# A transformer block with polymax attention: the first attention iteration started from SBUF

## The reference

```python
x = x + 0.5 * ffn(layernorm(x))
x = x + attn(layernorm(x), W_attn, W_proj)
x = x + 0.5 * ffn(layernorm(x))
# ffn(x)  = x @ W.T + b + (x @ V_r) @ C.T          256 -> 256, rank 32
# attn(x) = y @ W_proj, 16 heads of 16 numbers, causal, no softmax but
# polymax(s) = (s*s + 1)/1000 for s > 0, (1 - s/100)/1000 for -100 <= s <= 0, else 0
```

## Time and profile before

| | us |
|---|---|
| median of 3 runs | 1990.86 (1988.06 to 1992.23) |
| the profiled execution, its own time | 1981.72 |
| its span in the profile | 1980.0 |
| PE / DVE / ACT / POOL busy | 1641.8 / 1264.8 / 1335.6 / 1325.6 |
| start of iteration 1 (first raise of its half 0) | 284.0 |
| start of iteration 2 | 390.1 |

### The profile page before, as it was taken

The page is one execution under the profiler, slowest core; times in us unless marked ns, Lnnn a source line. Parts: engine busy times, 40 slices in busy tenths (PEclk is TensorE's granted clock), DMA queues, the critical chain, the costliest instruction groups (busy, mean ns, idle before and its releaser), DMA issues.

```text
span 1980.0 us, 64621 instructions
## 1 busy us (share of the span) xinstructions
PE 1641.8 (83%) x27158; PEld 764.4 (39%) x27158; DVE 1264.8 (64%) x2065; ACT 1335.6 (67%) x1634; POOL 1325.6 (67%) x1419
## 2 busy tenths in 40 slices
PE   4677789798989788898878889787988888888874
PEld 2443334343434344343434434343443333334332
DVE  2456676666666667666666756667666667667552
ACT  2244567787777676777667677767777787776560
POOL 3354567787777767677776767867676767676551
PEclk9898999999999999999999999999999999999996
DMA  2344332323334152333415233341513232314111
GB/s 84 112 147 127 109 127 61 117 78 103 93 92 122 42 161 64 103 90 98 127 42 160 65 97 96 94 119 43 144 60 117 69 82 63 108 37 113 36 36 57
DMA packets 155175, 183.00 MB, mean 92 GB/s; under 512 B 22012, under 2 KB 129660, under 8 KB 152836
## 3 DMA queue, kind: packets, MB, share of 16 engines
q1 hardware_dynamic: 154884, 178.82, 30.7%
HBM read 102.43 MB, written 76.30 MB: 90 GB/s over the span
## 4 chain that ended last, share of the span: by engine, by line
PE 56%; DVE 15%; issue 11%; ACT 10%; POOL 4%; DMA 2%; SPq 0%; DVEq 0%; ACTq 0%; POOLq 0%
PE y_ps L974 21%; PE score L974 19%; PE bank L974 13%; DVE rp L909 8%; ACT rp L818 3%; PE bank L1000 3%; ACT rp L838 3%; ACT rp L834 2%; POOL z L685 2%; DVE lin L915 2%; ACT lin L824 1%; DVE bnst_ln L934 1%; DVE qk_max L921 1%; DMA out_dram<-x 1%; DVE rest L454 1%
## 5 line engine op out<-in xcount | busy, mean ns | idle before, releaser
L909 DVE TENSOR_SCALAR rp<-score 128x1024 f32<-128x1024 f32 (+2 forms) x864 | 860.2, 1002 | 321.6 <-PE score L974 313.3
L974 PE MATMUL score<-qs,ks 96*32 96x512 bf16 (+3 forms) x10240 | 711.4, 354 | 237.0 <-DVE rp L909 126.4
L723 POOL TENSOR_TENSOR rp<-rp 128x1024 f32<-128x1024 f32 (+1 forms) x416 | 756.7, 1828 | 170.5 <-DVE rp L909 158.8
L818 ACT ACTIVATE rp<-score 128x1024 f32<-128x1024 f32 (+1 forms) x416 | 413.0, 993 | 340.9 <-PE score L974 338.0
L974 PE MATMUL y_ps<-rp,vt 128*16 128x512 f32 (+3 forms) x5120 | 598.4, 540 | 9.0 <-ACT rp L838 7.3
L974 PEld LDWEIGHTS score<-qs,ks 96*32 96x32 bf16 x10240 | 241.5, 96 | 648.1 <-DVE rp L909 338.7
L834 ACT ACTIVATE rp<-rp,rise 128x1024 f32<-128x1024 f32 (+1 forms) x416 | 456.1, 1119 | 1.4 <-POOL rp L698 1.4
L698 POOL TENSOR_SCALAR_AFFINE_SELECT rp<-rp 128x256 f32<-128x256 f32 (+1 forms) x384 | 184.0, 481 | 315.4 <-ACT rp L818 165.4
L838 ACT ACTIVATE rp<-rp 128x1024 f32<-128x1024 f32 (+2 forms) x224 | 290.4, 1298 | 112.9 <-DVE rp L909 64.6
L974 PEld LDWEIGHTS y_ps<-rp,vt 128*16 128x16 f32 x5120 | 138.4, 97 | 117.8 <-ACT rp L838 19.4
L974 PE MATMUL bank<-w_ffn,zT 128*32 128x256 f32 x2048 | 160.2, 404 | 7.6 <-ACT zT L779 7.6
(11 more groups left out here) (78 smaller groups left out, 1359.5 us busy)
## 6 DMA issues: line engine op xcount, KB each, us to landing
part_scratch<-parts SPq DMA_DIRECT2D x16, 1536.0 KB, 7.5
qs<-part_scratch SPq DMA_DIRECT2D x384, 64.0 KB
ks<-part_scratch SPq DMA_DIRECT2D x384, 64.0 KB, 2.3
state_scratch<-st_new SPq DMA_DIRECT2D x16, 528.0 KB
st<-state_scratch SPq DMA_DIRECT2D x64, 132.0 KB
x_sb<-in_L_attn_x_dram SPq DMA_DIRECT2D x16, 512.0 KB, 4.2
x_scratch<-x SPq DMA_DIRECT2D x16, 512.0 KB, 5.2
qT_scratch<-qkT SPq DMA_DIRECT2D x16, 512.0 KB, 3.8
```

The costliest lines, as they stand in the source:

```text
L723: pool.tensor_tensor(half, half, half, ALU.mult).then_inc(squared["pool"], 1)
L818: nc.scalar.activation(rp[T % RP_BUFS][:, 2:4, off:CH], score[H % S_BUFS][:, :, off:CH], ACT.Relu).then_inc(raised["act"], 1)
L909: nc.vector.tensor_scalar(rp[T % RP_BUFS][:, 2 * u:2 * u + 2, off:CH], score[H % S_BUFS][:, :, off:CH], 0.0, RISE, ALU.max, ALU.add).then_ ...
L974: return nc.tensor.matmul(*args, start=start, stop=stop, skip_group_check=True)
```

## The change

Four things. (1) In front of slot 0 each operand has a semaphore of its own: PE waits for the identity and the three FFN weights, which are loaded before the bias and the other weights; POOL makes the identity first; four fills (st_new, k_sb, qT, y_sb) go to DVE; ACT empties w_ffn only at the slot of the first z1T, and the wait for the constants moves there on ACT and DVE. (2) For the four chunks of iteration 0 the heads come straight from SBUF: 24 DMAs of 16 partitions for qs, 24 for ks, one for qT and one for vt; only st still goes through DRAM. From iteration 1 on the loads are the same as before, with separate semaphores for q, k, v, qT and st. (3) In the early stretches kT moves from slots 30 and 32 to 14 and 15, in front of the FFN of the next chunk, ffn and ln2 go 2 slots later, v 2 slots later, state to 32 to 35. (4) The halves of iteration 0 begin in s0: those of chunk c at slot 28 of the stretch sc, spread evenly until those of chunk c+1 begin; the last ones until iteration 1.

```diff
-A_EARLY = {"z1T": (12, 13), "ffn": (14, 18), "z2T": (38, 39), "ln1": 0, "ln2": 22}
-B_EARLY = {"qT": (0, 2), "k": (4, 8), "v": (22, 26), "kT": (30, 32), "state": (31, 33, 34, 35)}
+A_EARLY = {"z1T": (12, 13), "ffn": (16, 20), "z2T": (38, 39), "ln1": 0, "ln2": 24}
+B_EARLY = {"qT": (0, 2), "k": (4, 8), "kT": (14, 15), "v": (24, 28), "state": (32, 33, 34, 35)}
 C_SHORT = {"proj": (0, 4), "ln3": 8, "z3T": (20, 21), "out": (22, 26)}
+
+
+HALVES_AFTER = 28
...
+    def put_halves(self, slots):
+        for s in slots:
+            assert s not in self.halves
+            self.halves[s] = self.next_half
+            self.next_half += 1
...
-    at = o.stretch(40)
-    o.stage(0, at, B_EARLY)
-    o.stage(1, at, A_EARLY)
-    for c, (length, first) in enumerate(((40, 20), (40, 14), (44, 14), (48, 14))):
-        at = o.stretch(length, spread(first, length, 2 * (LAST[c] + 1 - FIRST[c])))
-        o.stage(c + 1, at, B_EARLY)
-        o.stage(c + 2, at, A_EARLY)
+
+    starts = []
+    for c, length in enumerate((40, 40, 40, 44, 48)):
+        at = o.stretch(length)
+        o.stage(c, at, B_EARLY)
+        o.stage(c + 1, at, A_EARLY)
+        starts.append(at + HALVES_AFTER)
+    starts[CPB] = o.n
+    for c in range(CPB):
+        o.put_halves(spread(starts[c], starts[c + 1], 2 * (LAST[c] + 1 - FIRST[c])))
...
-            sp.dma_start(w_in[:], ffn_w.rearrange("(k p) d -> p k d", p=P)).then_inc(w_loaded, 16)
             sp.dma_start(x_sb[:], x_d[0:CH, :].rearrange("(i p) d -> p i d", p=P)).then_inc(x_loaded, 16)
-            sp.dma_start(vr_in[:], ffn_v.rearrange("(k p) r -> p k r", p=P)).then_inc(w_loaded, 16)
-            sp.dma_start(c_in[:], ffn_c.rearrange("(k p) r -> p k r", p=P)).then_inc(w_loaded, 16)
-            sp.dma_start(bias_half[:], ffn_b.rearrange("(a n) -> a n", a=1).broadcast_to([P, DM])).then_inc(w_loaded, 16)
-            sp.dma_start(w_qkv[:], w_attn.rearrange("(k p) n -> p k n", p=P)).then_inc(w_loaded, 16)
-            sp.dma_start(w_out[:], w_proj.rearrange("(k p) n -> p k n", p=P)).then_inc(w_loaded, 16)
-
-            sp.wait_ge(const_ready, 5)
+            sp.dma_start(vr_in[:], ffn_v.rearrange("(k p) r -> p k r", p=P)).then_inc(ffn_loaded, 16)
+            sp.dma_start(c_in[:], ffn_c.rearrange("(k p) r -> p k r", p=P)).then_inc(ffn_loaded, 16)
+            sp.dma_start(w_in[:], ffn_w.rearrange("(k p) d -> p k d", p=P)).then_inc(ffn_loaded, 16)
+            sp.dma_start(bias_half[:], ffn_b.rearrange("(a n) -> a n", a=1).broadcast_to([P, DM])).then_inc(bias_loaded, 16)
+            sp.dma_start(w_qkv[:], w_attn.rearrange("(k p) n -> p k n", p=P)).then_inc(qkv_loaded, 16)
+            sp.dma_start(w_out[:], w_proj.rearrange("(k p) n -> p k n", p=P)).then_inc(out_loaded, 16)
+
+            sp.wait_ge(filled, 1)
             for b in range(BATCH):
                 sp.dma_start(st_d[b, 0], st_new[:, 0, :]).then_inc(st_zero, 16)
-            sp.wait_ge(st_zero, 16 * BATCH)
...
+            def first_heads(dst, c, j, split, where):
+
+                for r, which in enumerate(PAIRS):
+                    for u in range(QH):
+                        sp.dma_start(dst[HD * r:HD * r + HD, u, CH * c:CH * c + CH],
+                                     parts[HD * u:HD * u + HD, j, which[split], :]).then_inc(where, 16)
...
-                    if x.chunk < CPB:
-                        put(x.empty_at + 5, "kq", 0, x.chunk)
+
+                if x.chunk < CPB:
+                    if (x.kind, x.i) == ("qT", 0):
+                        put(x.empty_at + 2, "first q", x.chunk)
+                    if (x.kind, x.i) == ("kT", 0):
+                        put(x.empty_at + 2, "first k", x.chunk)
+                    if (x.kind, x.i) == ("v", 1):
+                        put(x.empty_at + 1, "first v", x.chunk)
+                    if (x.kind, x.i) == ("state", NB - 1):
+                        put(x.empty_at + 7, "first st", x.chunk)
...
-                    if what == "kq":
-                        n, c = args
-                        all_stored(c + 1)
-                        load_q(n, c, q_loaded[c])
-                        load_k(n, c, k_loaded[c])
+                    if what == "first q":
+                        c, = args
+                        cols = slice(CH * c, CH * c + CH)
+                        if c == 0:
+                            sp.wait_ge(filled, FILLED)
+                        wait_emptied(sp, "qT", c, 0)
+                        sp.dma_start(qT[1:QD + 1, cols], qkT[0:QD, 0, :]).then_inc(qT_loaded[c], 16)
+                        sp.wait_ge(split_step, 12 * c + 3)
+                        first_heads(qs, c, 0, 0, q_loaded[c])
+                    if what == "first k":
+                        c, = args
+                        sp.wait_ge(split_step, 12 * c + 9)
+                        first_heads(ks, c, KC, 1, k_loaded[c])
+                    if what == "first v":
+                        c, = args
+                        wait_emptied(sp, "v", c, 1)
+                        sp.dma_start(vt[:, NB * c:NB * c + NB, :], v_sb[:, 0, :, :]).then_inc(v_loaded[c], 16)
+                    if what == "first st":
+                        c, = args
+                        sp.wait_ge(st_zero, 16 * BATCH)
+                        sp.wait_ge(st_stored, (c + 1) * 16)
+                        load_st(0, c, st_loaded[c])
...
-            pool.memset(ident[:], 0.0).then_inc(const_ready, 1)
+            pool.memset(ident[:], 0.0).then_inc(ident_ready, 1)
+            pool.wait_ge(ident_ready, 1)
+            pool.affine_select(out=ident[:], in_=ident[:], compare_op=ALU.not_equal, fill=1.0, base=0,
+                               pattern=[[-1, P]], channel_multiplier=1).then_inc(ident_ready, 1)
             pool.memset(smask[:], SLOPE).then_inc(const_ready, 1)
-            pool.memset(st_new[:], 0.0).then_inc(const_ready, 1)
-            pool.memset(k_sb[:], 1.0).then_inc(const_ready, 1)
-            pool.memset(y_sb[0][:], 0.0).then_inc(const_ready, 1)
-            pool.memset(qT[:], 1.0).then_inc(const_ready, 1)
             pool.memset(slope_mask[:], SLOPE).then_inc(const_ready, 1)
...
-            pool.wait_ge(w_loaded, 16 * 6)
-            pool.wait_ge(const_ready, 14)
-            pool.tensor_scalar(bias_half[:], bias_half[:], 0.5, 0.0, ALU.mult, ALU.add).then_inc(const_ready, 1)
-            pool.wait_ge(const_ready, CONSTS)
+            pool.wait_ge(bias_loaded, 16)
+            pool.tensor_scalar(bias_half[:], bias_half[:], 0.5, 0.0, ALU.mult, ALU.add).then_inc(bias_loaded, 1)
+            pool.wait_ge(bias_loaded, 17)
...
+                        if a <= CPB:
+                            act.wait_ge(qT_loaded[a - 1], 16)
+                            act.wait_ge(q_loaded[a - 1], heads_loaded(0))
+                            act.wait_ge(k_loaded[a - 1], heads_loaded(0))
...
+                if s == o.place["z1T", 0, 0].empty_at:
+                    empty_weights()
...
-            dve.wait_ge(const_ready, CONSTS)
+            nc.vector.memset(st_new[:], 0.0).then_inc(filled, 1)
+            nc.vector.memset(k_sb[:], 1.0).then_inc(filled, 1)
+            nc.vector.memset(qT[:], 1.0).then_inc(filled, 1)
+            nc.vector.memset(y_sb[0][:], 0.0).then_inc(filled, 1)
...
-            pe.wait_ge(const_ready, CONSTS)
-            pe.wait_ge(w_loaded, 16 * 6)
+            pe.wait_ge(ident_ready, 2)
+            pe.wait_ge(ffn_loaded, 16 * 3)
...
-                    pe.wait_ge(q_loaded[c], (n + 1) * (16 * Q_LOADS))
+                    pe.wait_ge(q_loaded[c], heads_loaded(n))
                 if u == 0 and t == KEY_FIRST[kb // NB]:
-                    pe.wait_ge(k_loaded[kb // NB], (n + 1) * (16 * K_LOADS))
+                    pe.wait_ge(k_loaded[kb // NB], heads_loaded(n))
...
+                if t == KEY_FIRST[kb // NB]:
+                    pe.wait_ge(v_loaded[kb // NB], (n + 1) * 16)
                 if t == FIRST[c]:
+                    pe.wait_ge(qT_loaded[c], (n + 1) * 16)
+                    pe.wait_ge(st_loaded[c], (n + 1) * 16)
```

More of the change, by code:

```diff
@@ L153, in stage @@
                 self.jobs.append(Job(kind, chunk, i, at + start))
+    def put_halves(self, slots):
[3 more added lines that the diff above has]
+            self.next_half += 1
     def stretch(self, length, slots=()):
-        for s in slots:
-            self.halves[self.n + s] = self.next_half
-            self.next_half += 1
+        self.put_halves([self.n + s for s in slots])
         at = self.n
@@ L356, in build @@
         bank = [ps(f"bank{i}", [P, CH]) for i in range(2)]
-        w_loaded = sem("w_loaded")
+        ffn_loaded = sem("ffn_loaded")
+        bias_loaded = sem("bias_loaded")
+        qkv_loaded = sem("qkv_loaded")
+        out_loaded = sem("out_loaded")
+        ident_ready = sem("ident_ready")
+        filled = sem("filled")
         const_ready = sem("const_ready")
@@ L385, in build @@
         q_loaded = [sem(f"q_loaded{c}") for c in range(CPB)]
+        v_loaded = [sem(f"v_loaded{c}") for c in range(CPB)]
```

(45 more changed lines are left out.)

12 lines of the change are left out of this document (5 added, 7 removed).

## The result

The changed kernel takes 2041.65 us (median of 4 runs, 2041.07 to 2041.78) against 1989.78 for the kernel before: ratio 1.026, 95% interval 1.025 to 1.028. The forecast was 1982.9, the range 1966 to 1998. The profiled execution spans 2040.0 us against 1980.0. Iteration 1 starts at 344.3 us, not 284.0, and from there to the end both take the same, 1695.7 and 1696.0 us. So all of the +60 us lies where the change was made. The medians differ by 52 us only, because the profiled execution of the kernel before was 8 us faster than its median; no trace shows where these 8 us lie.

A forecast was written before the change was run, and what follows sets the result against it. PE with its waits was taken to set the pace. Setup -10.0, removals -24.1, additions +6.6, +4, +1.5 and +14 gave -8.0 us: 1973.7 in the profiled execution, 1982.9 against the median; range 1966 to 1998.

The forecast's parts named there:

- The prediction's rule: Time of stretches s0 to s4: PE busy time over 0.861, PE's busy share in iteration 1, plus named waits.
- (a): In s0, the keys' 24 issues take 11.0 us, so PE waits 6.6 us for them at slot 64.
- (c): PE waits for st through DRAM before first values of chunks 1 to 3: 2, 8 and 4, sum 14 us.
- What goes: Waits removed by the new order in the stretches before iteration 1: -24 us, bounds -13 to -28.
- The two waits behind ACT: PE waits behind ACT's qT copy, held by the parts store; both vanish, 9.7 us.
- step (b): z2T behind the keys: ln2 and z come late, adding 4 us in s0 and 1.5 in s1.
- the DVE jam: At the stretch's end kT splits meet state sums on DVE; moving the splits away gains 3 us.
- Setup: Ahead of s0, z1T starts at 13.8 us, not 23.76: -10.0 us, bounds -8.5 to -11.
- the exchange: Rival: SP becomes the narrow place and the next x chunk comes late; sum +1, 1992 us, chance 0.19.
- The slow rival: State waits through DRAM cost 25.5 us, not 14; sum +3.5, with key wait at its bound 1996; chance 0.25.

The follow-up runs named there:

- issue_forms: The kernel before with 60 DMAs added on SP behind its last store, in five forms; 0.59 to 0.60 us an issue SBUF to SBUF, 0.42 to 0.43 with DRAM.
- act_shares: The changed kernel, but ACT issues 12 of each burst of 24 direct loads; 2014.38 us, 1.011.
- kT_first_only: The changed kernel's setup and new order of jobs, with loads through DRAM and halves at the slots of the kernel before; 1975.66 us, 0.994.
- halves_late: The changed kernel with the halves of iteration 0 back at the slots of the kernel before (96, 130, 170, 214); 2008.61 us, 1.009.
- act_shares_46: The changed kernel with ACT issuing half of each direct-load burst and halves beginning 46 slots behind the stretch's start, not 28; 2002.81 us, 1.007.
- setup_only: The changed kernel with everything but the setup put back as in the kernel before; 1980.71 us, 0.995.

## Why the prediction was wrong

The sum was -8.0 us; the traces have +60.3. The prediction's rule (busy / 0.861 + named waits) held: by it the changed stretches should take 201.4 / 0.861 = 233.9 us and the named waits: z 3.74 + 5.18 + 3.53 + 2.23 + 4.62 = 19.3, keys 30.3, state 25.2. The sum is 308.7; measured were 310.8. Waits under 2 us and those for DVE (up to 3.46 us) are not counted, as they were not in the prediction. What failed are the sizes of its terms, one wait that it let the halves cover, and a term, the clock, that it did not have.

1. **(a), the price of an issue.** The step took 0.46 us from a DRAM load and said "the issue cost hardly depends on size". That is right, but it depends on the kind: 0.63 us from start to start for SBUF to SBUF (issue_forms). 24 x 0.63 = 15.1 us, not 11.0. And the step forgot the queue in front: two bursts and a store are 32 us in a row, where the splits that release them are only 12 us apart. In s0 the splits were done 18.9 us into the stretch, as forecast (19.0), but the keys waited 5.5 us for the queue and 4.3 us more for their own issues. Key waits 30.3 us against 6.6 forecast, in three stretches, not one; act_shares takes 24.6 of them away by sharing the queue.
2. **(c), the state.** 25.2 us against 14. The way in the prediction (POOL behind masks and a square, store, load) is what the traces show, but SP's backlog came on top. For chunk 2 PE stood from 198.5; the last sum ended at 202.1, the store was issued at 204.1, the load at 208.6, and PE went on at 210.9. For chunk 1 the wait was 0, not 2; PE had stood for 9.10 us at the keys earlier in s1.
3. **The clock.** The sum had no term for it. With PE idle for 29.4, 20.6 and 26.6 us in s0 to s2 (8.5, 10.5 and 14.1 before) the granted clock fell from 0.85 to 0.91 down to 0.74 to 0.76, and PE was busy 13.0 us longer with the same work, 15.1 us by the rule.
4. **What goes.** The two waits behind ACT went (9.7 us), as forecast. The halves were to cover z in front of z1T in s2, s3 and s4, 11.4 us. In s3 and s4 they nearly did (0.21 and 1.77 us are left), but in s2 3.03 became 4.62, and in s1 1.58 became 3.53. With s0 (3.74) and z in front of z2T, step (b) (5.18 + 2.23 = 7.4 against 5.5), 19.3 us of z stand against the 4 + 5.5 left in the forecast. kT_first_only shows why even the 9.7 are worth less than they look: z, whose chain on DVE and POOL does not start earlier, is waited for instead. Of the 3 us booked for the DVE jam, 1.8 can be found (waits for DVE over 0.9 us add up to 9.9 us, 11.8 before).
5. **Setup.** 6.5 us in this profile, not 10.0. w_in landed at 8.39 us, 6.0 after its issue behind x; the step took 3.9. PE then went from the fold into z1T without a gap, as the step had it, and z1T began 7.7 us earlier than before. Another 1.2 us went between z1T and s0, where the FFN matmuls took 6.25 us, not 5.03, at a granted clock of 0.83 in place of 0.88.

Sum by terms: +15.1 clock, +30.3 keys, +25.2 state, +2.3 z (19.3 against 17.0, with the 1.58 of s1), -9.7, -6.5 setup, together +56.7 of the +60.3. Against the forecast: keys +23.7, clock +15.1, state +11.2, z +9.8, setup +3.5, and the 3.0 for DVE, which the rule cannot show, together 66.3 of the 68.3 us between -8.0 and +60.3.

The rival that came nearest is the exchange: SP became the narrow place, and the Trainium skill's page DMA: Bandwidth & Descriptors, section Rules for kernel authors (coalesce small transfers, below 64 KB mostly overhead), pointed the right way, and in issue_forms 16 KB cost an issue as long as 64 KB. I priced it at +1 because I let the x load alone be late. In halves_late just this mechanism, with x waited for by up to 18.9 us and the parts store by up to 15.6, costs 33 us. The slow rival, state waits at their upper price of 25.5, was right in size (25.2), but it was held to be alternative to the others, and they came together.

What stays open: how the 71 us of early halves with DRAM loads divide between waits and clock; no run holds the clock fixed. And whether direct loads would pay if one DMA could carry what 24 do was not tried. Neither the direct loads nor the early halves were run with the old order of jobs.

## What to carry to other kernels

Before a transfer is cut into many small ones, multiply their number by the issue time of that very kind, and write down the whole queue of the issuing engine for one period, with everything that stands behind; an issue that runs from SBUF to SBUF cost 0.63 us here, with 16 partitions as with 64. Work that is moved forward in an in-order engine must be placed behind the time at which its operands can be there at all: at 28 slots, 24 us into s0, PE met keys that SP had there only after 41 us from SBUF and 35 us through DRAM (31 with half of the issues on ACT), and stalled with everything behind it. And when one wait is removed, name the next one on the same engine before booking the gain: here it took back about half.

## What the runs showed of the hardware

- An issue on SP took 0.59 us from SBUF to SBUF and 0.42 with DRAM on either side, each plus 0.04; 16 or 64 partitions, 16 or 64 KB made a difference of 0.01 (issue_forms, one execution). On ACT's queue 11 such issues took 7.01 us, 0.64 each, and ACT's own work stood still meanwhile: its copy of k waited 7.07 us (act_shares_46). Right behind a burst in the changed kernel, stores to DRAM took 0.58 us too (57.26 and 73.19 us).
- Behind large transfers issues took longer: six loads after the parts store and the x transfers took 6.20 us, up to 1.8 each (changed kernel, 132.8 us), where six took 2.70 in the kernel before.
- The granted clock was low where PE stood idle most: 0.74 in s0, with 29.4 of 57 us without a matmul, 1.00 in iteration 1. Idle time alone does not give it: in s1 PE was idle for 10.5 us of 37.7 at 0.91 in the kernel before, and for 9.9 of 40.5 at 0.83 in setup_only.
